# Moving residual products to the start of two graph attentions, with interleaved sums and turned tiles

## What is computed

```python
x = x + gnn(layernorm(x), edges)
x = x + ffn(layernorm(x))            # causal attention with 12 heads, then the best of 8 experts for each token

def gnn(x):
    h = relu(layer_norm(gat(x, W1, 4 heads of 256), g1, be1)) + (x @ Wr1 + br1)    # x @ Wr1: "res1", 625 x 1024
    return layer_norm(gat(h, W2, 1 head of 768), g2, be2) + (h @ Wr2 + br2)        # h @ Wr2: "res2", 625 x 768

def gat(x, W):
    xl = x @ W
    # for each edge: leaky_relu(a_src . xl[src] + a_dst . xl[dst]), a softmax over the edges of each
    # destination, and the sum of xl[src] weighted with it, plus a bias
```

## Time and profile before

| | us |
|---|---|
| median of 3 runs | 1158.85 |
| lowest and highest | 1154.31, 1162.18 |
| the profiled execution | 1158.79 |
| its span | 1156.7 |
| PE busy in the span | 1051.2 |
| DVE busy | 743.6 |
| ACT busy | 559.0 |
| POOL busy | 193.5 |

### The profile page before, as it was taken

The page is one execution under the profiler, slowest core; times in us unless marked ns, Lnnn a source line. Parts: engine busy times, 40 slices in busy tenths (PEclk is TensorE's granted clock), DMA queues, the critical chain, the costliest instruction groups (busy, mean ns, idle before and its releaser), DMA issues.

```text
span 1156.7 us, 19050 instructions
## 1 busy us (share of the span) xinstructions
PE 1051.2 (91%) x6176; PEld 658.3 (57%) x6177; DVE 743.6 (64%) x1327; ACT 559.0 (48%) x741; POOL 193.5 (17%) x182
## 2 busy tenths in 40 slices
PE   5998768999969699999989669999999999999997
PEld 3555457745746476556677525555555555555554
DVE  6677768793545554528988588971116988989511
ACT  2677556500331124428873446861116877878411
POOL 2000000092005513108000120201001210204000
PEclk9999979999979899997999679999999999999999
DMA  8300010021500830011012659991004999999300
GB/s 300 98 0 1 31 78 1 1 92 53 127 0 2 174 56 1 1 39 68 2 42 96 216 207 375 353 359 33 6 18 157 395 358 390 364 375 375 118 16 3
DMA packets 92144, 155.60 MB, mean 135 GB/s; under 512 B 36388, under 2 KB 36468, under 8 KB 92095
## 3 DMA queue, kind: packets, MB, share of 16 engines
q1 hardware_dynamic: 89694, 149.20, 37.2%
q0 software_dynamic: 2400, 5.77, 1.4%
HBM read 153.21 MB, written 7.77 MB: 139 GB/s over the span
## 4 chain that ended last, share of the span: by engine, by line
PE 76%; DVE 12%; issue 4%; DMA 3%; ACT 3%; DVEq 1%; POOL 1%; SPq 0%; ACTq 0%; POOLq 0%
PE psum L1397 32%; PE psum L1617 17%; PE psum L1592 16%; PE psum L1386 2%; PE psum L1434 2%; PE psum L1601 2%; DMA low<-in_x_dram 1%; DMA low<-in_L_ffn_W_dram 1%; DVE area L1267 1%; PE psum L1513 1%; PE psum L1588 1%; DVE low L1078 1%; DVE low L1079 1%; PE psum L1449 1%; ACT low L866 1%
## 5 line engine op out<-in xcount | busy, mean ns | idle before, releaser
L1267 DVE TENSOR_TENSOR area<-low,area 128x1536 f16<-128x1536 f32 x144 | 245.7, 1753 | 12.4 <-ACT area L911 11.9
L1397 PE MATMUL psum<-area,low 128*125 128x512 f16 (+4 forms) x1116 | 245.6, 381 | 4.6 <-DVE low L1254 2.6
L1592 PE MATMUL psum<-area,low 128*128 128x512 f16 x972 | 220.5, 381 | 0.0
L1617 PE MATMUL psum<-area,low 128*128 128x384 f16 x1296 | 219.2, 327 | 0.0
L911 ACT ACTIVATE area<-low 128x1536 f16<-128x1536 f32 x138 | 200.4, 1484 | 33.6 <-DMA low<-in_L_ffn_W_dram 27.1
L1397 PE MATMUL psum<-area 125*128 125x64 f16 (+10 forms) x1452 | 199.0, 291 | 8.2 <-DVE area L1238 3.7
L1397 PEld LDWEIGHTS psum<-area,low 128*125 128x125 f16 (+2 forms) x1116 | 143.4, 141 | 101.6 <-issue 60.7
L1617 PEld LDWEIGHTS psum<-area,low 128*128 128x128 f16 x1296 | 127.3, 98 | 80.6 <-issue 1.7
L1397 PEld LDWEIGHTS psum<-area 125*128 125x128 f16 (+3 forms) x1452 | 129.0, 124 | 61.8 <-issue 12.7
L1592 PEld LDWEIGHTS psum<-area,low 128*128 128x128 f16 x972 | 95.5, 98 | 113.7 <-issue 2.7
L922 ACT ACTIVATE low<-psum 128x512 f32<-128x512 f32 x54 | 31.9, 591 | 160.8 <-PE psum L1592 157.7
(11 more groups left out here) (223 smaller groups left out, 1204.9 us busy)
## 6 DMA issues: line engine op xcount, KB each, us to landing
low<-in_L_ffn_W_dram SPq DMA_DIRECT2D x144, 768.0 KB, 8.0
area<-in_L_gnn_W_dram SPq DMA_DIRECT2D x2, 3072.0 KB, 12.0
area<-in_L_gnn_Wr_dram SPq DMA_DIRECT2D x2, 3072.0 KB, 16.3
area<-in_L_ffn_Wv_dram SPq DMA_DIRECT2D x6, 384.0 KB, 6.4
area<-in_L_ffn_Wq_dram SPq DMA_DIRECT2D x6, 384.0 KB, 6.3
area<-in_L_ffn_Wk_dram SPq DMA_DIRECT2D x6, 384.0 KB, 6.8
area<-in_L_ffn_Wp_dram SPq DMA_DIRECT2D x2, 1152.0 KB, 7.2
low<-in_x_dram SPq DMA_DIRECT2D x5, 375.0 KB
```

What stands on the lines that cost most here:

```text
L1267: dve.tensor_tensor(low_, raw_view(u), high_, ALU.subtract).then_inc(low_ok, 1)
L1397: ins = pe.matmul(place(name)[0:parts, at:at + w], left(q), right(q)[:, at:at + w], start=(q == 0), stop=(q == k - 1))
L1592: ins = pe.matmul(psum[:, (c % 2) * BANK:(c % 2 + 1) * BANK], ht[x_][:, k, :], w1_s[c][w_][:, k, :], start=False, stop=(k == KD - 1 and x_ ...
L1617: ins = pe.matmul(psum[:, (4 + q) * BANK:(4 + q) * BANK + D // 2], hidT[c % 2][x_][:, j, :], w2_s[c][w_][:, j, q * D // 2:(q + 1) * D // 2 ...
```

## The change

The product of tile 0 of `res1` is made at the beginning of the layer 1 attention: its first bank ahead of the row of source values, its second bank behind it. ACT copies it out of PSUM to a spare place (`res1_early`), from where DVE reads it later. The products of tiles 0 and 1 of `res2` are made at the beginning of the layer 2 attention: the first bank of tile 0 ahead of the source row, the rest behind it. ACT scales and copies them to `res2_early`. With that, the split of Wv moves: its high part on ACT goes ahead of layer 2's attention, its low part on DVE goes into step 3 of the loop. The second load of x is issued when the last negative maximum of layer 2 is there, and each tile is loaded in two pieces (112 and 13 rows) instead of one. In the join of layer 1 DVE takes the low parts of turned tiles between the last sums, and `NORM_ORDER` and DVE's order in the norm stage are rearranged.

```diff
-NORM_ORDER = (("res2", 0), ("res2", 1), ("hT", 0), ("res2", 2), ("V", 0), ("hT", 1), ("res2", 3), ("hT", 2),
-              ("res2", 4), ("V", 1), ("hT", 3), ("V", 2), ("hT", 4), ("V", 3), ("V", 4))
+EARLY_RES2 = 2
+NORM_ORDER = (("res2", 2), ("hT", 0), ("res2", 3), ("hT", 1), ("V", 0), ("hT", 2), ("res2", 4), ("hT", 3), ("V", 1),
+              ("V", 2), ("hT", 4), ("V", 3), ("V", 4))
...
+        res1_early = low[0:P, TW + 4 * N:TW + 4 * N + HC]
+        res2_early = [A(0, KD * D + t * D, D, P) for t in range(EARLY_RES2)]
...
-            done(sp, ("agg", 2, T - 1))
-            for t in range(T):
-                sp.dma_start(total[:, t, :], x[t * P:(t + 1) * P, :]).then_inc(x2_in, 16)
+            sp.wait_ge(neg_ok, (HEADS + 1) * T)
+            for t in range(T):
+                for r0, r1 in ((0, 112), (112, P)):
+                    sp.dma_start(total[r0:r1, t, :], x[t * P + r0:t * P + r1, :]).then_inc(x2_in, 16)
...
                     xl2_copy(T - 1)
+                    weights_high(wv_in, staged[:, 0:KD * D], wv_parts)
...
+                    if layer == 1 and i == 2:
+                        copy(("res1", 0), res1_early, place(("res1", 0), HC, P))
+                    if layer == 2 and i == 2:
+                        for t in range(EARLY_RES2):
+                            done(act, ("res2", t))
+                            emptied_by(("res2", t), act.activation(res2_early[t], place(("res2", t), D, P), ACT.Copy,
+                                                                   scale=1.0 / SCALE_UP))
                     if i >= 2:
                         probT_copy()
...
-            done(act, ("agg", 2, T - 1))
-            weights_high(wv_in, staged[:, 0:KD * D], wv_parts)
...
+                    if layer == 2 and i == 3:
+                        weights_low(1, staged[:, 0:KD * D], wv_parts)
...
+            def residual_row(t):
+                if t == 0:
+                    was_emptied(dve, ("res1", 0))
+                    link(dve.tensor_tensor(res1[:, 0, :], res1_early, row1["br1"], ALU.add))
+                else:
+                    done(dve, ("res1", t))
+                    emptied_by(("res1", t), dve.tensor_tensor(res1[:, t, :], place(("res1", t), HC, P), row1["br1"], ALU.add))
...
+            for t in range(T - 1):
+                residual_row(t)
+                join_residual(t)
+            residual_row(T - 1)
+            h1T_low(0)
+            join_residual(T - 1)
+            h1T_low(1)
+            h1T_low(2)
+            graph_low(2, wr2_parts)
+            h1T_low(3)
+            h1T_low(4)
...
             def residual_norm(t):
+                if t < EARLY_RES2:
+                    was_emptied(dve, ("res2", t))
+                    link(dve.tensor_tensor(total[:, t, :], res2_early[t], total[:, t, :], ALU.add))
...
-            for t in (0, 1):
-                residual_norm(t)
+            residual_norm(0)
+            residual_norm(1)
             hT_lows(0)
             residual_norm(2)
-            V_low(0)
             hT_lows(1)
             residual_norm(3)
+            V_low(0)
             hT_lows(2)
             residual_norm(4)
+            hT_lows(3)
+            weights_low(2, staged[:, 0:KD * D], wq_parts)
             V_low(1)
-            weights_low(2, staged[:, 0:KD * D], wq_parts)
-            hT_lows(3)
...
             pe.wait_ge(wr1g_in, 16)
-            for t in range(T):
-                product(("res1", t), ...)
+            by_x0(0, 0, BANK, False)
+            graph_attention(1, HEADS, HID, xl1, lambda: by_x0(0, BANK))
+            for t in range(1, T):
+                by_x0(t)
...
-            graph_attention(2, 1, D, xl2)
             pe.wait_ge(g_low, 2)
+            by_h1("res2", 0, wr2_parts, 0, BANK, False)
+            def early_residuals():
+                by_h1("res2", 0, wr2_parts, BANK)
+                for t in range(1, EARLY_RES2):
+                    by_h1("res2", t, wr2_parts)
+            graph_attention(2, 1, D, xl2, early_residuals)      # called right behind the matmuls of src_row
```

More of the change, by code:

```diff
@@ L43, in item_plan @@
                 plan.append((("src_row", layer, 0), "A"))
+                plan += [(("res2", t), "A") for t in range(EARLY_RES2)] if layer == 2 else [(("res1", 0), "A")]
             elif i % T == T - 2 and i // T + 1 < heads:
@@ L50, in item_plan @@
         if layer == 1:
-            plan += [(("res1", t), "D") for t in range(T)]
+            plan += [(("res1", t), "D") for t in range(1, T)]
     plan += [(name, "A" if name[0] == "hT" else "D") for name in NORM_ORDER]
@@ L761, in graph_high, with weights_high @@
                 act.activation(high_low[0], staged, ACT.Copy, scale=SCALE_UP).then_inc(g_high, 1)
+            def weights_high(loaded, whole, high_low):
+                act.wait_ge(loaded, 16 * KD)
+                act.activation(high_low[0], whole, ACT.Copy, scale=SCALE_UP).then_inc(w_high, 1)
             for layer, heads in ((1, HEADS), (2, 1)):
@@ L1066, in source_diagonals, with weights_low @@
                 ins.then_inc(row_ok, 1)
+            def weights_low(n, whole, high_low):
+                dve.wait_ge(w_high, n)
+                dve.scalar_tensor_tensor(out=high_low[1], in0=whole, scalar=SCALE_UP, in1=high_low[0], op0=ALU.mult,
+                                         op1=ALU.subtract).then_inc(w_low, 1)
             def graph_attention(layer, heads, width, agg, bias_row, behind=None):
@@ L1149, in _ @@
             normal2(T - 1)
[L1151 to L1154, removed]
             def hT_lows(t):
@@ L1388, in turn, with product @@
                 ins.then_inc(made, 1)
-            def product(name, k, left, right, width, parts):
-                free(pe, name)
-                at = 0
+            def product(name, k, left, right, width, parts, first=0, whole=True):
+                if first == 0:
+                    free(pe, name)
+                at = first
                 while at < width:
@@ L1399, in product @@
                     at += w
-                ins.then_inc(made, 1)
+                if whole:
+                    ins.then_inc(made, 1)
             pe.wait_ge(bounds_v, 1)
@@ L1438, in _, with graph_attention @@
                 pe.matmul(high, zero16[:, 0:P], zero16[:, 0:N - BANK], start=False, stop=True).then_inc(made, 1)
-            def graph_attention(layer, heads, width, xl):
+            def graph_attention(layer, heads, width, xl, behind=None):
                 n_, before_ = heads * T, 0 if layer == 1 else HEADS * T
@@ L1451, in graph_attention @@
                         ins.then_inc(made, 1)
+                    if i == 0 and behind:
+                        behind()
                     if 1 <= i <= n_:
@@ L1459, in graph_attention, with by_x0, by_h1 @@
                                 lambda k: xl[:, k, h * width:(h + 1) * width], width, P)
-            graph_attention(1, HEADS, HID, xl1)
+            def by_x0(t, first=0, width=HC, whole=True):
+                product(("res1", t), KD, lambda k: aT6[:, k, t * P:(t + 1) * P], lambda k: wr1_g[:, k, :], width, P,
+                        first, whole)
             pe.wait_ge(wr1g_in, 16)
-            for t in range(T):
-                product(("res1", t), KD, lambda k: aT6[:, k, t * P:(t + 1) * P], lambda k: wr1_g[:, k, :], HC, P)
+            by_x0(0, 0, BANK, False)
+            graph_attention(1, HEADS, HID, xl1, lambda: by_x0(0, BANK))
+            for t in range(1, T):
+                by_x0(t)
             pe.wait_ge(g_low, 1)
-            def by_h1(name, t, high_low):
+            def by_h1(name, t, high_low, first=0, width=D, whole=True):
                 product((name, t), 3 * KH, lambda k: h1T[PARTS[k % 3][0]][:, k // 3, t * P:(t + 1) * P],
-                        lambda k: v3(high_low[PARTS[k % 3][1]], KH)[:, k // 3, :], D, P)
+                        lambda k: v3(high_low[PARTS[k % 3][1]], KH)[:, k // 3, :], width, P, first, whole)
             for t in range(T + 1):
```

27 lines of the change are left out of this document (12 added, 15 removed).

## The result

The changed kernel takes 1133.93 us (median of 4 runs, 1131.86 to 1134.42) where the old one takes 1158.34 us (4 runs); the ratio is 0.9773, with a 95% interval of 0.9752 to 0.9794. The forecast was 1133.

A forecast was written before the change was run, and what follows sets the result against it. PE was taken to bound nearly throughout, except where the chain leaves it. Layer 1 opening 2.2, its end 9.0 and norm stage 14.6 (layer 2 opening's 1.5 included) made 25.8 us off 1158.8: 1133, range 1122 to 1144.

The forecast's parts named there:

- All four places: PE's idle gaps at both attention openings, end of layer 1, load of x, and Wq split at the norm stage's end.
- The opening: Layer 1 attention's start: early `res1` product fills PE's gaps at full clock; gain 2.2 us, bounds 0 and 2.9.
- The end of layer 1: Behind layer 1's attention: first `xl2` product starts 9.0 us earlier, POOL and DVE next late; bounds 6 and 14.1.
- Walking both queues: Behind layer 1's attention: POOL and DVE wait for each other's SBUF reads; POOL's last sum ends at 270.5, 1.9 later.
- The list of signs: Closing list of what traces would show, including filled gaps, full clock, and DVE's row sum of tile 0 near 2 us.
- the price of the shared reading: End of layer 1: without the SBUF port lock of DVE and POOL the gain would be 11.0 instead of 9.0.
- Layer 2's opening: Layer 2 attention's start: early `res2` products delay the first `agg`; cost 1.5 us, bounds 0 and 4.7.
- Norm stage: Load of x leaves the chain, POOL's rows next late; `V` of tile 3 gains 14.6 us, bounds 10 and 19.5.
- PE's list: Norm stage, `hT` of tile 0 to `V` of tile 3: 39.0 us plus 0.6 waiting for a slot, before 46.9.
- The first: Rival: shared SBUF reading costs less, PE alone sets layer 1's end or POOL is not late; 1126, chance 0.18.
- The second: Rival: layer 2's attention becomes bound by ACT and DVE, POOL's layer 1 chain is delayed; 1141, chance 0.16.
- The third: Rival: early products run at the lower clock in both openings, together 32 us; 1165, chance 0.02.

The follow-up runs named there:

- e4: Old kernel with matmuls whose results are unread put into PE's gaps at both attention openings, nothing moved; 1152.71 us, ratio 0.9944.
- e2: Changed kernel with all five `res1` products back behind the layer 1 attention, new order of low parts kept; 1142.55 us, ratio 0.9837.
- e3: Changed kernel with half of the `res1` product steps of tiles 1 to 4 left out; 1134.64 us, ratio 0.9782.
- e9: Changed kernel with DVE adding br1 to the early `res1` product in place, in step 3 of the layer 1 attention; 1131.64 us, ratio 0.9758.
- e8: Changed kernel with the old load of x: issued after layer 2's last `agg`, one piece a tile; 1140.38 us, ratio 0.9849.
- e10: Changed kernel with g2 and be2 of layer 2's last row applied by DVE, not POOL, ahead of that row's residual sum; 1130.39 us, ratio 0.9744.
- e1: Old kernel with only the earlier, two-piece load of x and the moved split of Wv; 1149.6 us, ratio 0.9913.
- e6: Changed kernel with g2 and be2 of layer 2's last row applied by DVE in its wait for POOL's small instructions; 1132.53 us, ratio 0.9765.
- e5: Changed kernel with DVE's sum of `res1` tile 0 moved into its wait for POOL's root; 1132.94 us, ratio 0.9786.
- e12: Changed kernel unaltered, run again beside its variants; 1131.91 us, ratio 0.9760.

## Why the prediction was right

**What bounds.** All four places where the old chain left PE closed as stated: gaps of 3.88 and 6.61 us in layer 1 became none and 1.45, those of layer 2, 4.08 and 5.64, both none, with 0.39 us left ahead of the first `agg`.

**Layer 1.** The opening gave 2.2 us. It is the clock's: e4, which moves nothing, gives 3.3 there, and the early product costs 1.1 of them. The end of layer 1 gave 9.1 against 9.0: not the 10.3 of a product off PE, because the POOL and DVE chain is next late. e2 and e3 bracket it: more PE work lengthens the stage, less doesn't shorten it. Walking both queues, each engine waiting for the other's running instruction, gave POOL's end at 46.1 us behind the first `res1` product (270.5 less 224.4), and it came at 46.1 (269.8 less 223.7). The list of signs had a mistake: it expected DVE's sum of tile 0 near 2 us, while the walk that ends at 270.5 needs it at 3.3 (1.1 and POOL's 2.2 ahead of it), and it took 3.36. And the price of the shared reading in this term, 2.0 us (11.0 less 9.0), was not borne out as far as it was tested: with the early sum taken out of POOL's way (e9) the stage gives 10.1 us, 1.0 more. POOL's last two row instructions take 3.36 and 3.21 us in the changed kernel where they took 2.34 and 2.35, those before them what they took; in e9 one of the two is back at 2.35. The other is lengthened by a join that in the old kernel still waited for PE, and no run takes that away.

**Layer 2's opening.** A cost of 1.6 against 1.5. What the prediction gave as one number is two: 4.3 us of delay behind the early products and 2.8 us back from the clock (e4).

**Norm stage.** Removing the 17 us load gave 9.5 us at `hT` of tile 0 where 8.8 were forecast, since POOL's four rows stand in its place; e8 shows the load's share, e10 the share of the last row. POOL's fourth ended 12.5 us behind the last `agg`, not 13.2. Behind `hT` PE's list took 38.6 us against 39.6; the slot that was to be emptied 0.6 us late was not: DVE was ahead.

**Where it met by offsets.** Five stretches are off by 0.7 to 1.7 us, three towards faster (1.7, 0.7 and 1.1) and two towards slower (1.5 and 0.8), which leaves 1.1 us in the sum. That 1133 lies within 1 us of the median is in part luck. The new `NORM_ORDER` and DVE's new order in the norm stage were never run without the rest, so their share of the 38.6 us is not known.

**Rivals.** The first, that PE would be next late, is out by e3 for layer 1 and by e10 for the norm stage. The second, that layer 2's loop becomes bound by ACT and DVE, is out: behind the first, the `agg` products of layer 2 and their transposes follow each other without a gap, and POOL's last row in layer 1 was not later than walked. The third, low clock in the openings, is out by the windows.

**What was not forecast** is small: the first `xl2` product at full clock, which gave 1.7 us in the profiled execution of the changed kernel and is chance (below: the same kernel profiled again had it at the lower clock), and +1.5 and +0.8 us in stretches that the change does not touch; they also differ between the executions of the variants (the last stretch is 708.8 us in e1 and 712.0 in e2).

## What to carry to other kernels

Price a moved piece of work against the second-latest chain, not against its own length: here 10.3 us of PE work moved away were worth 9.1, a load of 17 us was worth 10 alone, and each number came from walking the next queue. An engine's gap at the start of a pipelined loop can take independent work cheaply (10.7 us of `res1` for 1.1 us of delay in layer 1, 15.6 us of `res2` for 4.3 in layer 2) if that work comes in pieces around the small item the loop waits for, and the clock it keeps up pays part of the rest. When a residual is copied out of PSUM to free the slot, the sum that follows has two SBUF operands and takes turns with GpSimd: do it while GpSimd is idle (1.0 us in e9's trace).

## What the runs showed that I had not expected

A GpSimd instruction on one or five elements a partition waits for the end of a DVE instruction with two SBUF operands, like a large one: 0.22 and 0.57 us became 0.81 and 1.25 us beside DVE sums (e6, one element), and 0.24 became 1.10 (e5, five).

The same code with the same gap of PE can find either level of the clock. In the changed kernel PE waits 3.25 us ahead of the first `xl2` product, which then took 8.02 us. The same kernel profiled again (e12) had a gap of 3.26 us there, and the product took 9.70 us; in e6 and e8, with gaps of 3.26 and 3.25 us, it took 10.91 and 9.39 us:

The lines are of e6 and of e12.

```profile
269.82 10.91 PE L1442 MATMUL psum<-area,low 128*125 128x512 f16 x48 [3.26 <-DVE low L1155]
```

```profile
268.34 9.70 PE L1433 MATMUL psum<-area,low 128*125 128x512 f16 x48 [3.26 <-DVE low L1155]
```

Between these executions this alone is worth up to 2.9 us, more than the 2.7 us that the two late improvements bring together.
